# Gathered expert outputs scaled by ScalarE and added by GpSimd in layer 1's time mixing, in place of one fused VectorE operation

## The reference, cut to what matters

```python
# layer 0, last sublayer: two of eight experts for each row
out = jnp.einsum('eth,te->th', y, combine)         # y: expert outputs, combine: the two probabilities of a row
x = x + out
# layer 1, first sublayer: on layernorm(x)
xk = x * time_mix_k + shifted * (1.0 - time_mix_k) # likewise xv, xr
k, v, r = xk @ Wk.T, xv @ Wv.T, sigmoid(xr @ Wr.T)
# for each time step: running maximum pp, running sums aa, bb
p = maximum(pp, u + k); e1 = exp(pp - p); e2 = exp(u + k - p)
out = (e1 * aa + e2 * v) / (e1 * bb + e2)
x = x + (r * out) @ Wo.T
```

## Time and profile before

| what | value |
|---|---|
| median of 3 timed runs | 3090.8 us (3089.63 to 3092.59) |
| span of the profiled execution | 3157.6 us |
| TensorE busy over the span | 2733.3 us, 87% |
| VectorE busy | 2058.2 us, 65% |
| ScalarE busy | 1649.1 us, 52% |
| GpSimd busy | 714.3 us, 23% |
| the stage of the change | about 1547 to 2034 us of the span |

### The profile page before, as it was taken

One profiled execution on the slowest core, in us unless ns is written; L12 is line 12 of the kernel. 1 busy time (PEld: TensorE's weight loads), 2 busy tenths in 40 slices (PEclk: granted clock), 3 DMA queues, 4 the chain that ended last, 5 costly groups with the idle time before them and its releaser, 6 DMA issues. The chain is left out here.

```text
span 3157.6 us, 57839 instructions
## 1 busy us (share of the span) xinstructions
PE 2733.3 (87%) x20742; PEld 2084.7 (66%) x20743; DVE 2058.2 (65%) x3869; ACT 1649.1 (52%) x2861; POOL 714.3 (23%) x690
## 2 busy tenths in 40 slices
PE   8999889996776899999689999688888888476899
PEld 6777644454665788888677787555555555365788
DVE  5666648886233232111389999689999999676544
ACT  3333357775222222222256666499999999588000
POOL 0111104444455000000333321122222220200600
PEclk9999889998887899999899999799999999799999
DMA  3000252223555444444411110000110000144554
GB/s 127 1 1 1 77 189 84 83 82 121 200 174 186 150 140 143 143 145 137 140 42 41 39 37 20 22 23 28 28 29 28 28 28 21 42 198 188 195 190 146
DMA packets 131042, 291.61 MB, mean 92 GB/s; under 512 B 21008, under 2 KB 57872, under 8 KB 122128
## 3 DMA queue, kind: packets, MB, share of 16 engines
q1 hardware_dynamic: 104336, 228.99, 21.2%
q0 software_dynamic: 17792, 51.40, 4.9%
q10 hardware_dynamic: 8704, 8.39, 0.8%
HBM read 184.90 MB, written 103.81 MB: 91 GB/s over the span
## 5 line engine op out<-in xcount | busy, mean ns | idle before, releaser
L1293 ACT ACTIVATE cx_h<-bank,c_b 128x256 f32<-128x256 f32 (+1 forms) x288 | 117.6, 459 | 387.7 <-PE bank L1245 387.7
L1952 DVE TENSOR_SCALAR e_low<-bank 128x2048 f32<-128x2048 f32 x128 | 293.3, 2292 | 30.2 <-PE bank L1845 30.2
L1245 PE MATMUL bank<-cx_zT,cx_w 128*128 128x256 f32 (+1 forms) x1152 | 249.6, 370 | 2.0 <-DMA cx_w<-cw_dram 1.1
L1827 ACT ACTIVATE e_low<-e_low 128x2048 f32<-128x2048 f32 x128 | 244.7, 1912 | 4.1
L1256 PE MATMUL bank<-c_w,cx_h 128*128 x1088 | 246.6, 379 | 0.0
L1825 ACT ACTIVATE e_low<-e_low 128x2048 f32<-128x2048 f32 x128 | 243.6, 1903 | 0.0
L2319 PE MATMUL bank<-wout,fd_q 128*128 128x256 f32 x1024 | 223.2, 381 | 20.6 <-DVE fd_q L2338 20.6
L1245 PEld LDWEIGHTS bank<-cx_zT,cx_w 128*128 128x128 f32 x1152 | 211.6, 192 | 30.0 <-DMA cx_w<-cw_dram 1.5
L2319 PEld LDWEIGHTS bank<-wout,fd_q 128*128 128x128 f32 x1024 | 195.9, 191 | 47.8 <-DVE fd_q L2338 20.9
L1256 PEld LDWEIGHTS bank<-c_w,cx_h 128*128 128x128 f32 x1088 | 201.2, 190 | 24.4
L1845 PE MATMUL bank<-e_qT,e_kT 32*128 32x256 f32 x2048 | 148.8, 404 | 67.9 <-DVE e_high L1953 67.1
(11 more groups left out here) (375 smaller groups left out, 6402.5 us busy)
## 6 DMA issues: line engine op xcount, KB each, us to landing
cx_w<-cw_dram SPq DMA_DIRECT2D x72, 512.0 KB, 3.3
hidden<-fu_h SPq DMA_DIRECT2D x32, 1024.0 KB, 3.9
fd_h<-hidden SPq DMA_DIRECT2D x32, 1024.0 KB, 5.1
cx_rows<-expert_rows SPq DMA_DIRECT2D x64, 256.0 KB, 3.2
slot_y<-cx_y POOLq DMA_DIRECT2D x64, 256.0 KB, 2.6
g_cT<-ctxT_dram SPq DMA_DIRECT2D x32, 256.0 KB, 5.0
queries<-g_qT SPq DMA_DIRECT2D x32, 256.0 KB, 5.8
b_qT<-queries SPq DMA_DIRECT2D x32, 256.0 KB
```

What stands on the lines that cost most here:

```text
L1245: last = nc.tensor.matmul(H[k][f // 2][:, (f % 2) * GROUP_ROWS:(f % 2) * GROUP_ROWS + cols], w1[k][:, c, f * P:(f + 1) * P], zT[k][:, c, 0 ...
L1827: nc.scalar.activation(flat(low[n % RING][:]), flat(low[n % RING][:]), ACT.Exp, scale=-1.0).then_inc(low_ready, 1)
L1952: nc.vector.tensor_scalar(flat(low[n % RING][:]), HEADS4.rearrange("p r s -> p (r s)"), -1.0, 0.0, ALU.mult, ALU.max).then_inc(neg_ready, 1)
```

## The change

ScalarE multiplies each gathered tile in place by its probability (`weigh`), two choices by two tiles, so four instructions for each batch. It does so one batch further ahead than the row statistics: `weigh(b+5)` stands in iteration b between `root(b+4)` and `exponentials(b)`. GpSimd adds the scaled tiles to X, two instructions of 512 values for each batch (`collect`), the second after the first. It places the addition of batch b-1 after the gathers of batch b. VectorE keeps the statistics, and waits for GpSimd's second addition ahead of them. Batches 0 to 3 stay with VectorE as before. Before the loop ScalarE scales batch 4. The two tiles of a choice become one buffer. In the diff the first `collect`, with the loop behind it, is GpSimd's, `weigh` is ScalarE's, and the second `collect` and `statistics` are VectorE's; the latter holds the two L1684 and the two L1687. VectorE calls `collect` only for batches 0 to 3 now.

```diff
+            def collect(b):
+                x = t["X"][:, b * TB:(b + 1) * TB, :]
+                pool.wait_ge(weighed, CHOSEN * TB * (b - AHEAD + 1))
+                nc.gpsimd.tensor_tensor(x, x, chosen_y[b % RING][0][:], ALU.add).then_inc(pool_first, 1)
+                pool.wait_ge(pool_first, b - AHEAD + 1)
+                nc.gpsimd.tensor_tensor(x, x, chosen_y[b % RING][1][:], ALU.add).then_inc(pool_second, 1)
+
             for b in range(B):
-                if b >= RING:
+                if b >= AHEAD + RING:
+                    pool.wait_ge(pool_second, b - RING - AHEAD + 1)
+                elif b >= RING:
                     pool.wait_ge(second_in, TB * (b - RING + 1))
...
+                if b > AHEAD:
+                    collect(b - 1)
+            collect(B - 1)
...
+            def weigh(b):
+                act.wait_ge(chosen_in[b % RING], 16 * CHOSEN * TB * (b // RING + 1))
+                for c in range(CHOSEN):
+                    for n in range(TB):
+                        y, tile = chosen_y[b % RING][c][:, n, :], b * TB + n
+                        nc.scalar.activation(y, y, ACT.Copy, scale=t["prob"][:, c, tile:tile + 1]).then_inc(weighed, 1)
...
             turned(1)
+            weigh(AHEAD)
             for b in range(B + 1):
                 if known(b):
                     receptance(b)
                     exponents(b)
                 if known(b + AHEAD):
                     root(b + AHEAD)
+                if known(b + AHEAD + 1):
+                    weigh(b + AHEAD + 1)
                 if known(b):
                     exponentials(b)
...
             def collect(b):
-                tiles = range(b * TB, (b + 1) * TB)
...
-                        nc.vector.scalar_tensor_tensor(x, chosen_y[b % RING][c][n][:], t["prob"][:, c, tile:tile + 1], x, ALU.mult, ALU.add).then_inc(done, 1)
+                        nc.vector.scalar_tensor_tensor(x, chosen_y[b % RING][c][:, n, :], t["prob"][:, c, tile:tile + 1], x, ALU.mult, ALU.add).then_inc(done, 1)
+                statistics(b)
+
+            def statistics(b):
+                if b >= AHEAD:
+                    dve.wait_ge(pool_second, b - AHEAD + 1)
                 for n in tiles:
-                    dve.wait_ge(second_in, n + 1)
+                    if b < AHEAD:
+                        dve.wait_ge(second_in, n + 1)
...
                 if known(b + AHEAD):
-                    collect(b + AHEAD)
+                    statistics(b + AHEAD)
```

More of the change, by code:

```diff
@@ L1428, in layer1_rwkv @@
         shift, decay = sb("shift", [P, NT]), sb("decay", [P, DC, S])
-        chosen_y = [[[sb(f"chosen{k}{c}{n}", [P, D]) for n in range(TB)] for c in range(CHOSEN)] for k in range(RING)]
+        chosen_y = [[sb(f"chosen{k}{c}", [P, TB, D]) for c in range(CHOSEN)] for k in range(RING)]
         spread, moments, log_var, rstd = sb("spread", [P, NT, 6]), sb("moments", [P, NT, 2]), sb("log_var", [P, NT]), sb("rstd", [P, NT])
@@ L1441, in layer1_rwkv @@
         names = ("w_in", "setup", "wexp", "consts", "weights", "shift", "z", "zT_raw", "zT", "k_raw", "v_raw", "r_raw", "pp", "h", "arg", "ex", "abs", "er",
-                 "ev", "state", "prod", "nd", "whole", "ln", "gate_in", "gate", "y", "o_raw", "x_done", "first", "second", "spread", "moments", "log_var", "rstd")
+                 "ev", "state", "prod", "nd", "whole", "ln", "gate_in", "gate", "y", "o_raw", "x_done", "first", "second", "weighed", "pool_first", "pool_second", "spread", "moments", "log_var", "rstd")
         (w_in, setup, wexp, consts, weights, shift_ready, z_ready, zT_raw, zT_ready, k_raw, v_raw, r_raw, pp_ready, h_ready, arg_ready, ex_ready, abs_ready, er_ready,
-         ev_ready, state_ready, prod_ready, nd_ready, whole_ready, ln_ready, gate_in, gate_ready, y_ready, o_raw, x_done, first_in, second_in, spread_ready, moments_ready, log_var_ready, rstd_ready) = (sem(n) for n in names)
+         ev_ready, state_ready, prod_ready, nd_ready, whole_ready, ln_ready, gate_in, gate_ready, y_ready, o_raw, x_done, first_in, second_in, weighed, pool_first, pool_second, spread_ready, moments_ready, log_var_ready, rstd_ready) = (sem(n) for n in names)
         chosen_in = [sem(f"chosen_in{k}") for k in range(RING)]
@@ L1469, in _ @@
                     for n in range(TB):
-                        pool.indirect_dma_start(chosen_y[b % RING][c][n][:], None, t["slot_y"],
+                        pool.indirect_dma_start(chosen_y[b % RING][c][:, n, :], None, t["slot_y"],
                                                 bass.IndirectOffsetOnAxis(ap=t["slot"][:, c, b * TB + n:b * TB + n + 1], axis=0)).then_inc(chosen_in[b % RING], 16)
+                if b > AHEAD:
+                    collect(b - 1)
+            collect(B - 1)
         @block.scalar
@@ L1680, in collect @@
                             dve.wait_ge(first_in, b * TB + n + 1)
-                        nc.vector.scalar_tensor_tensor(x, chosen_y[b % RING][c][n][:], t["prob"][:, c, tile:tile + 1], x, ALU.mult, ALU.add).then_inc(done, 1)
+                        nc.vector.scalar_tensor_tensor(x, chosen_y[b % RING][c][:, n, :], t["prob"][:, c, tile:tile + 1], x, ALU.mult, ALU.add).then_inc(done, 1)
+                statistics(b)
+            def statistics(b):
+                tiles = range(b * TB, (b + 1) * TB)
+                if b >= AHEAD:
+                    dve.wait_ge(pool_second, b - AHEAD + 1)
                 for n in tiles:
-                    dve.wait_ge(second_in, n + 1)
+                    if b < AHEAD:
+                        dve.wait_ge(second_in, n + 1)
                     nc.vector.bn_stats(spread[:, n, :], t["X"][:, n, :]).then_inc(spread_ready, 1)
```

## The result

The changed kernel takes **3101.76 us** (median of 6 runs, 3099.5 to 3102.87) against 3091.84 us for the kernel before (6 runs): +9.9 us by these medians. The ratio on record is 1.0036, with a 95% interval of 1.0026 to 1.0046. The forecast was 3098.6 us, +7.8. The direction held, and so did the loop that sets the batch; the sum fell some 2 us short, and one premise, on contention, was false.

The account below looks back on a forecast made before the run. VectorE sets 13.74 us a batch now; with the scalings a loop through ScalarE and VectorE bounds it at 12.45 + 1.60 = 14.05. The sum of +7.8 us on 3090.8 gives 3098.6 us, range 3085 to 3109.

Parts of the forecast that it names:

- The loop behind VectorE: From M, the start of VectorE's scans, through ScalarE's exponentials and logarithm to gates and next M: 12.45 us, 14.05 with scalings.
- TensorE's place: Transposes start at M + 6.90, earlier than before; TensorE stays 0.6 us clear of the path and does not lengthen the loop.
- The price W of the scalings: Four ScalarE scalings between root and exponentials take W = 1.60 us a batch, bounds 1.20 to 1.96.
- Place, not amount: ScalarE idles 5.10 us a batch in front of L1504, but the scalings are put inside the loop and lengthen it.
- Cover of GpSimd's additions: GpSimd's sums end about 6 us before VectorE's statistics want them, so the additions stay hidden.
- The sum: +1.6 us for batches 0 and 1, +7.8 for batches 2 to 26, -1.6 at the end: +7.8 us.
- The start, not in the sum: Breaking the row of gathers ahead of the first scans could move M0 5.0 us earlier or 3.7 later; taken as 0.
- Rival A: With the scalings off the loop TensorE becomes the bound at 12.95 us a batch, total 3069 us; chance 0.13.
- Rival B: Scalings cheap, W near 1.30, or the start 5 us shorter: no change, 3088 to 3094 us; chance 0.22.
- Rival C: GpSimd's additions hold VectorE beyond its new wait, 0.3 to 0.4 us a batch, adding 9 us: 3108 us; chance 0.08.
- costed at nothing: Contention for SBUF between GpSimd and VectorE: only GpSimd gives way, so 0 us in the sum.

Follow-up runs that it names:

- e10: Changed kernel with GpSimd's additions cut to one value in place of 256 from each tile; 3169.43 us, kernel before timed beside it 3164.83 us.
- e3: Changed kernel with four more scalings of the same shape per batch at the same place, output unused; 3140.89 us.
- e1: Changed kernel with the scalings of batch b+5 moved to the head of ScalarE's iteration b; 3083.17 us, ratio 0.9970.
- e0: The kernel before, unchanged, profiled once more; 3085.18 us.
- e9: e8 with the addition of add(b-2) alone moved in front of ratio(b-1), its statistics left behind; 3056.76 us, ratio 0.9889.
- e4: Changed kernel without ScalarE's scalings for batches 4 to 31, GpSimd's additions waiting for the gathers alone; 3091.18 us, ratio 1.0005.
- e6: e1 with GpSimd's additions held back by a wait until y of an earlier batch is made; 3074.92 us, ratio 0.9955.
- e5: e2 with GpSimd's additions cut to one value in place of 256 from each tile; 3063.38 us.
- e7: e6 with VectorE's whole add(b-2), statistics included, in front of ratio(b-1); 3087.88 us, ratio 0.9994.
- e8: e6 with the hold on GpSimd's additions counted one batch earlier; 3067.16 us, ratio 0.9922.
- e11: The kernel before with only e9's order on VectorE, the addition of b-2 in front of ratio(b-1); 3161.45 us, ratio 0.9995.
- e2: Changed kernel with the scalings moved behind the logarithm of b-1, in front of the normalisation; 3109.03 us, ratio 1.0053.

## Why the prediction was right, by its steps

**The loop behind VectorE: right.** The terms were 2.17, 0.03, 2.63, 0.42, 1.60, 1.90, 0.65 and 4.63. (The forecast 12.45 + 1.60 rounds their sum of 14.03 up.) In the timeline after they are 1676.71 - 1674.51 = 2.20 up to ScalarE's start, 1679.78 - 1676.71 = 3.07 (forecast 2.63 + 0.42 = 3.05), 1.60, 1683.27 - 1681.38 = 1.89, 0.64 and 1688.62 - 1683.91 = 4.71. The last is 0.08 above the forecast. The second scan of `states` is 1.25 long where it was 1.20; with the gathers shifted in e10 it is 1.20 and the batch 14.06. So about 0.05 of the 0.06 that my 14.05 lacked goes with the gathers, which now start together with that scan. TensorE's place was right too: the transposes start at 1681.40, M + 6.89 (forecast 6.90), and ScalarE's wait for `h`, 0.56 us, is the 0.6 by which TensorE was to be clear of the path.

**The price W of the scalings: right.** 1.60 us, by L206's row. e3 is the direct test: a second set of four added 1.59 us to each batch. The Trainium skill, "ScalarE: Activation LUTs", section "What ACT_TABLE_LOAD costs", gives 186 ns + 0.833 ns for each element and 93 ns for a pointer operand, which makes an estimate of 492 ns here; the trace agrees, L1504 has a median of 492 ns.

**Place, not amount: right.** The same four instructions in front of L1524 gave 18.6 us back (e1). ScalarE's load is the same in both.

**Cover of GpSimd's additions: right for the timing.** VectorE waited for a sum only in batch 0 (3.54 us), and that batch is longer by just the W that was forecast.

**The sum.** By the scans, with e0 as the kernel before:

| stretch | before (e0), us | after, us | difference | forecast |
|---|---|---|---|---|
| stage's first load to first scans | 27.35 | 28.39 | +1.0 | 0 |
| batch 0 | 16.55 | 18.15 | +1.6 | +1.6 with batch 1 |
| batch 1 | 13.05 | 14.10 | +1.05 | |
| batches 2 to 26 | 345.10 | 352.68 | +7.6 | +7.8 |
| batch 27 to last scans | 52.20 | 50.63 | -1.6 | -1.6 |
| sum | 454.25 | 463.95 | +9.7 | +7.8 |

The timed runs give +9.9. Two differences in the table are not the change's.

- The start, +1.0. The first fused multiply-add comes 11.57 us after the stage's first load in e0 and 12.29 in the changed kernel, but 12.30 in the first profile of the kernel before. The rest goes with TensorE's granted clock, which rises from the lower level 24.6 us after that load in e0 and 26.0 in the changed kernel; in e9, which has scalings and additions too, it rises after 24.7 and the first scans come at 27.40.
- Batch 3 of e0, 1.7 us too long (15.49 where its neighbours take 13.81). TensorE stood 2.89 us for bank T, its granted clock was then 0.50 from 1546.1 to 1549.5, and in batch 3 it was busy without a gap. Half of 3.4 us is the 1.7 (an estimate from these two rows). PEclk is the third number from the end:

```profile
core 0: us, PE busy (x) PEld busy (x) DVE busy (x) ACT busy (x) POOL busy (x), PEclk, DMA share, GB/s
1546.10:1549.50 3.40, 3.40 (x11) 2.83 (x10) 3.40 (x7) 1.82 (x4) 0.40 (x1) 0.50 0.22 68
1551.09:1566.58 15.49, 15.49 (x75) 13.61 (x74) 13.63 (x25) 8.65 (x17) 4.14 (x4) 1.00 0.12 35
```

The changed kernel has such a stretch too (1547.1 to 1550.5) and no long batch after it: its batches leave TensorE 1.3 us to spare. e4 and e6 have such a stretch and a batch 3 of 15.49 as well; e5, e7, e8 and e9 have neither. Without it batches 2 to 26 differ by 9.3 us, so that this row comes so near to its forecast is luck. Without both the change costs 9.7 - 1.0 + 1.7 = 10.4 us by the profiles, against the 7.8 forecast. The 2.6 us are 25 batches of 0.06, 1.5 us, and batch 1. There the prediction took L1504 of batch 1 for the anchor, 15.17 us after M0 and 2.9 behind the M of that batch (12.32), from a profile in which TensorE's granted clock was 0.76 over batch 0. In e0 and in the changed kernel alike it comes at 17.73, but M of batch 1 is at 16.55 in e0 and at 18.15 in the changed kernel: there the loop holds from batch 1 on, and adds 1.05 us.

**The start, not in the sum: right to take 0.** In e10, the changed kernel with small additions, the first scans come 40.26 us after the first load, with the 11.3 us wait; in e11, which has the unbroken row of gathers, 40.33, and in the first profile 40.21. The broken row moved the start by nothing.

**Rival A (TensorE the bound, 12.95 us):** wrong for the change, and its number was right for the kernels in which the scalings are off the loop: 12.95 in e5 and e8. Its condition was misstated: by the prediction's own terms 12.45 + W falls below 12.95 only for W under 0.5, not under 1.30, where the loop merely falls below VectorE's 13.74.

**Rival B (a cheap scaling or a shorter start):** wrong on both counts, W was 1.60 and the start did not move. The 0.30 that spoke for it came from L637, which reads a bank of PSUM and not SBUF as the scalings do.

**Rival C, and the contention "costed at nothing": the step that was weak.** The sum came out since the additions fall into VectorE's wait in the changed kernel; e10 shows that they cost 0.05 us a batch at most. They end 0.33 us before the first VectorE operation with two SBUF inputs, L1721, starts. But the reason that I gave, that GpSimd alone gives way, is false. I had drawn it from a gather beside L1648, and a gather is no addition: the additions hold a VectorE operation with two inputs from SBUF by 1.0 us (e1, e2), up to 1.6 (e4). The Trainium skill, "GPSIMD Engine Reference", Key points, names this case: GpSimd contends with VectorE instructions that have two SBUF inputs. The runs agree, and I should have given its rule a place in the sum by VectorE's timeline. Had the additions fallen elsewhere, the forecast would have been off by some 1.0 us x 26 = 26 us for each operation held, as mine for e1 and e2 were, by 12 and 38 us.

## What to carry to other kernels

Work taken from the busiest engine pays only if it is put where the receiving engine idles: ScalarE was idle for 37% of a batch, and the four instructions still cost their full 1.6 us each batch, because they were put between an input's arrival and the result that another engine waits for. Before moving work, write down the loops through two engines that hide just below the present bound, here 12.45 us under 13.74. When elementwise work goes to GpSimd, look at what VectorE does at that moment, and hold the GpSimd work by a semaphore until VectorE's operations have at most one input in SBUF; together with the right order this made a loss of 0.4% into a gain of 1.1%.

## What the runs showed of the hardware that was not expected

- A GpSimd addition of 512 float32 values (1.28 us alone) and a VectorE operation with two SBUF inputs take turns. The VectorE operation is longer by what was left of the addition when it started, less about 0.1 us: 0.14 to 1.64 us were seen, also for an operation on 2 values (0.15 us alone, 1.20 beside an addition). The addition is itself drawn out to 1.6 or 2.1. Beside scans and subtractions with one whole input in PSUM neither is longer (1.26, 0.88 and 1.27).
- GpSimd's gathers cost VectorE's operations hardly anything (1.25 in place of 1.20 for a scan, 1.21 as ever for L1673 in e8), though they themselves grow from 0.95 to as much as 2.0 us, as the one beside that L1673 does.
- An operation that is free to run early can be worse than one that is held: e4 with no scalings at all is 24 us slower than e8, which has them.
- A stretch of 3.4 us at TensorE's lower granted clock cost the kernel before 1.7 us, one batch later, and the changed kernel nothing that its batches show (14.11 each): there TensorE had time in hand.
